# Pairwise feature interaction in fp32 on one core: transposes and weighing of a group issued together, last four rows stored by single partitions, other slot counts

## The reference

```
bilinear = jnp.einsum('bie,ied->bid', feature, weight)
out      = jnp.einsum('bid,bjd->bij', bilinear, feature)
```

## Time and profile before

| | |
|---|---|
| median of three runs | 1572.7 us |
| the profiled execution | 1573.6 us |
| its span, first to last instruction | 1571.8 us |
| TensorE matmul busy | 1525.3 us, 97% |
| VectorE busy | 1145.3 us, 73% |
| ScalarE busy | 928.2 us, 59% |
| DMA, mean busy share of the 16 engines | about 90% |
| HBM read, written | 108 MB, 328 MB |
| TensorE clock granted | 0.996 of full speed |

### The profile page before, as it was taken

How to read it: one execution, slowest core, us unless ns; L and a number is a source line. 1 busy time by engine, 2 the same in 40 slices (tenths; PEclk the granted TensorE clock), 3 DMA queues, 4 the chain that set the end, 5 groups by cost and what they waited for, 6 DMA issues and landing times.

```text
span 1571.8 us, 40835 instructions
## 1 busy us (share of the span) xinstructions
PE 1525.3 (97%) x16192; PEld 1209.0 (77%) x16192; DVE 1145.3 (73%) x2048; ACT 928.2 (59%) x1313; POOL 0.7 (0%) x6
## 2 busy tenths in 40 slices
PE   8999999999999999999999999999999999999974
PEld 6888778877788777887778877788777887788753
DVE  0567777777777778678787687777777777786896
ACT  5666556655566655665556655566555665556532
POOL 0000000000000000000000000000000000000000
PEclk9999999999999999999999999999999999999998
DMA  9788999889989999989999899899999989999788
GB/s 234 226 270 267 297 295 282 280 268 293 296 275 288 281 293 283 292 275 277 288 289 292 274 281 296 275 289 280 290 290 283 286 273 290 288 280 289 239 266 248
DMA packets 294235, 438.51 MB, mean 279 GB/s; under 512 B 38049, under 2 KB 242849, under 8 KB 294049
## 3 DMA queue, kind: packets, MB, share of 16 engines
q1 hardware_dynamic: 294048, 435.92, 89.8%
HBM read 108.13 MB, written 327.68 MB: 277 GB/s over the span
## 4 chain that ended last, share of the span: by engine, by line
PE 88%; DVE 8%; issue 2%; DMA 1%; SPq 0%; ACT 0%; DVEq 0%
PE ps L219 49%; PE bp L203 24%; PE tp L187 14%; DVE staging L250 4%; DVE win L298 2%; DVE win L305 1%; PE ps L203 1%; PE ps L187 1%; DMA x<-feature_dram 0%; DMA out_dram<-staging 0%; DVE win L306 0%; SPq L138 0%; SPq L131 0%; ACT staging L250 0%; ACT bl L272 0%
## 5 line engine op out<-in xcount | busy, mean ns | idle before, releaser
L219 PE MATMUL ps<-win,bl 64*100 64x200 f32 x8192 | 932.3, 354 | 24.1 <-DVE staging L250 23.9
L219 PEld LDWEIGHTS ps<-win,bl 64*100 64x100 f32 x8192 | 699.7, 207 | 167.6 <-issue 164.7
L250 DVE COPY staging<-ps 100x800 f32<-100x800 f32 x512 | 505.8, 988 | 326.7 <-PE ps L219 324.6
L272 ACT COPY bl<-bp 128x512 f32<-128x512 f32 x384 | 322.3, 839 | 449.7 <-PE bp L203 449.7
L250 ACT COPY staging<-ps 100x800 f32<-100x800 f32 x512 | 423.1, 826 | 164.9 <-PE ps L219 162.9
L203 PE MATMUL bp<-xt,w 64*64 64x128 f32 x6144 | 419.7, 276 | 0.0
L203 PEld LDWEIGHTS bp<-xt,w 64*64 64x64 f32 x6144 | 326.8, 133 | 83.5 <-ACT xt L263 78.7
L298 DVE COPY win<-xt 128x400 f32<-128x400 f32 x512 | 276.7, 541 | 63.4 <-ACT xt L263 47.5
L187 PE MATMUL tp<-ident,x 128*128 128x128 f32 x1536 | 252.8, 287 | 5.9 <-DMA x<-feature_dram 5.9
L187 PEld LDWEIGHTS tp<-ident,x 128*128 128x128 f32 x1536 | 161.6, 141 | 89.3 <-issue 89.1
L263 ACT COPY xt<-tp 128x512 f32<-128x512 f32 x384 | 226.6, 590 | 5.3 <-PE tp L187 5.3
(11 more groups left out here) (4 smaller groups left out, 0.4 us busy)
## 6 DMA issues: line engine op xcount, KB each, us to landing
out_dram<-staging SPq DMA_DIRECT2D x1024, 300.0 KB, 4.1
x<-feature_dram SPq DMA_DIRECT2D x400, 256.0 KB, 4.1
out_dram<-staging SPq DMA_DIRECT2D x512, 25.0 KB
w<-weight_dram SPq DMA_DIRECT2D x24, 128.0 KB, 5.6
w<-weight_dram SPq DMA_DIRECT2D x2, 64.0 KB, 4.4
```

The lines of the kernel that those rows point to most:

```text
L219: last = nc.tensor.matmul(ps[s % TILES][0:FH, h, F * b:F * (b + 1)], rows_of_bl(n, R * k + PB * i + b)[64 * h:64 * h + 64], win[64 * h:64 ...
L250: copy(staging[:, slot, :, :, :].rearrange("p b h j -> p h b j"), ps[s % TILES][0:FH, :, 0:PB * F].rearrange("p h (b j) -> p h b j", j=F)) ...
L272: nc.scalar.copy(group_of_bl(n, t), bilinear_tile(n, t).rearrange("p (c b) -> p c b", c=C)).then_inc(bl_stored, 1)
```

## The change

Five edits.

1. In a quad with preparation TensorE issues both score sets first, then the transposes, then the weighing.
2. The last four partitions are stored once for eight sets (REST = 8), by four transfers of one partition each with 16 pieces of 1600 B. Before it was once for two sets, by one transfer of four partitions. In both there are 512 such transfers with 25 KB each. Their landing semaphores now stand for eight slots.
3. OSLOTS goes from 12 to 16.
4. To make room, XSLOTS goes from 6 to 5 and WSLOTS from 4 to 3.
5. `store_bl` of an odd block walks through the group with the four features innermost, so that it reads PSUM with a step of 128 elements and writes four contiguous elements at a time. Before it read contiguously and wrote with a step of 128.

```diff
-    XSLOTS = 6
+    XSLOTS = 5
     TILES = 3
-    OSLOTS = 12
-    WSLOTS = 4
+    OSLOTS = 16
+    REST = 8
+    WSLOTS = 3
...
-        rest_written = [sem(f"rest_written{i}") for i in range(OSLOTS // 2)]
+        rest_written = [sem(f"rest_written{i}") for i in range(OSLOTS // REST)]
...
-            return bl[:, :, C * t:C * (t + 1)].rearrange("p b c -> p c b")
+            return bl[:, :, C * t:C * (t + 1)]
...
-                if s % 2:
+                if s % REST == REST - 1:
                     wait_staged(sp, s - 1)
-                    sp.dma_start(out_v[FA:FH, PB * (s - 1):PB * (s + 1), :],
-                                 staging[FA:FH, slot - 1:slot + 1].rearrange("p s b h j -> p (s b) (h j)")
-                                 ).then_inc(rest_written[slot // 2], 16)
+                    for p in range(FA, FH):
+                        sp.dma_start(out_v[p:p + 1, PB * (s + 1 - REST):PB * (s + 1), :],
+                                     staging[p:p + 1, slot + 1 - REST:slot + 1].rearrange(
+                                         "p s b h j -> p (s b) (h j)")
+                                     ).then_inc(rest_written[slot // REST], 16)
...
                     scores(n, k, 0)
+                    scores(n, k, 1)
                     if k in transposed_at and (n + 1) * NG + transposed_at[k] < BLOCKS * NG:
                         transposes((n + 1) * NG + transposed_at[k])
-                    scores(n, k, 1)
                     if k in weighed_at and n + 1 < BLOCKS:
                         bilinear(n + 1, weighed_at[k])
...
-                engine.wait_ge(rest_written[slot // 2], 16 * used)
+                engine.wait_ge(rest_written[slot // REST], 16 * (FH - FA) * used)
...
-                nc.scalar.copy(group_of_bl(n, t), bilinear_tile(n, t).rearrange("p (c b) -> p c b", c=C)
+                cells = "p (c b) -> p c b" if n % 2 == 0 else "p (c b) -> p b c"
+                nc.scalar.copy(group_of_bl(n, t), bilinear_tile(n, t).rearrange(cells, c=C)
```

More of the change, by code:

```diff
@@ L41, in feature_interaction @@
     assert 2 * E == 128 and B % NB == 0 and FH % C == 0 and NG <= QUADS and R == 2 * PB
-    assert PB * F <= 512 and C * NB == 512 and OSLOTS % 2 == 0
+    assert PB * F <= 512 and C * NB == 512 and OSLOTS % REST == 0 and (BLOCKS * SETS_B) % OSLOTS == 0
     feature_v = feature.rearrange("b f e -> b (f e)")
@@ L165, in _ @@
                 sp.wait_ge(out_written[slot], 16 * uses)
-                if slot % 2:
-                    sp.wait_ge(rest_written[slot // 2], 16 * uses)
+                if slot % REST == REST - 1:
+                    sp.wait_ge(rest_written[slot // REST], 16 * (FH - FA) * uses)
         @block.gpsimd
```

## The result

The changed kernel takes 1660.3 us, the median of four runs (1657.75 to 1671.62), against 1573.4 for the kernel before: a ratio of 1.057 with an interval of 1.052 to 1.062. It is 5.7% slower, where the prediction said 4% faster. The profiled execution spans 1660.5 us.

A forecast was written before the change was run, and what follows sets the result against it. TensorE's order of work was taken as the bound, with the DMA engines close behind. Terms -79 + 19 - 6 + 0.5 = -65.5 on a 1571.8 us span gave 1506, a median of 1507 us; range 1486 to 1525.

The forecast's parts named there:

- The order on TensorE: Score sets directly after one another in quads with transposes and weighing save 0.26 or 0.175 us each: -79 us.
- The drain's term: After TensorE ends, the last stores finish sooner if DMA keeps up: -6 us, bounds -8 and 0.
- WSLOTS 4 to 3: With three windows TensorE waits 1.3 us for window copies at each of 15 block ends: +19 us.
- ScalarE's other walk: ScalarE's `bl` copy of 1.07 us takes 0.59 to 1.07; covered by ScalarE's room, so 0 us.
- The sum without the rest stores: Total with rest stores costing nothing, DMA staying covered: 1507 us.
- The rest stores: Single-partition stores use 16 engines, each with 25 packets a quad, 2.18 us or 2.82 with a load; DMA stays covered.
- The rival on the other side: Rest stores run one packet after another, 1.39 us each: 2071 us, or about 1850 by the port limit; chance 6%.
- The engines' balance: Before, rest stores used four engines, carrying 28 output packets a quad against 24: 2.44 us a quad, 3.08 with a load.
- The DMA rival: All engines or memory limit the stretches where SP was behind, so DMA becomes the bound: 1545 us, chance 20%.
- XSLOTS: Feature slots 6 to 5: loads keep enough lead over store landing, small cost while block 0 is prepared: +0.5 us.

The follow-up runs named there:

- e9: The kernel before with the new order on TensorE and no rest stores (rows 96 to 99 of each half not written): 1486.6 us.
- i2: The changed kernel with its four rest stores in a row issued by GpSimd instead of SP, each reading 16 source partitions (wrong rows): 1507.4 us.
- e4: The changed kernel without any rest stores (4% of the output not written): 1506.7 us.
- i1: The changed kernel with its four single-partition rest stores in a row issued by GpSimd instead of SP, true source: 1624.6 us.
- e3: The changed kernel with the same four rest stores issued by SP, each reading 16 source partitions instead of one (wrong rows): 1660.1 us.
- e8: The changed kernel with one rest store of four partitions, 16 pieces each, once in eight sets, in place of four single-partition stores: 1742.1 us.
- g2: The kernel before with the new order on TensorE and its rest stores issued by ScalarE, one quad late, instead of SP: 1490.6 us.
- e5: The kernel before with the new order on TensorE and nothing else changed: 1542.0 us.
- e1: The changed kernel with the rest store of before (four partitions, four pieces each, after every second set): 1541.9 us.

## Why the prediction was wrong, point by point

- **The order on TensorE: right.** A quad takes 3.25 us as worked out. e9 is 86.5 us under the kernel before. Its drain, from TensorE's end (1475.09 + 3.28) to the end of the span at 1484.7, takes 6.3 us (6.5 in i2, with all stores), against 15.2 before. So 78 are left for the order, where I had 79. The drain's term was -6 and measures -9 here; in the changed kernel itself the drain takes 15.4 us, nothing less than before.
- **WSLOTS 4 to 3: right.** +19 forecast; e4 against e9 shows 20.0, though with both other slot counts and ScalarE's walk in it. The waits for VectorE's copies into `win` appear as said (34.5 us).
- **ScalarE's other walk: right to cost at nothing.** Its copy fell from 1.07 us to 0.586, and ScalarE wasn't the bound.
- **The sum without the rest stores: right.** 1507 forecast, 1506.7 in e4, and 1507.4 in i2 with all stores but another source.
- **The rest stores: the step that failed.** It read "On 16 engines each has 25 packets a quad: 2.18 us without and 2.82 with a load". I had the number of engines right (44,192 packets against 44,193 forecast). But I gave a piece out of one partition the 0.087 us of any other piece, and I gave the issue nothing at all. In its place i1 and i2 show that this source costs 117 us in 512 stores, 0.23 us a store. And e3 against i2 shows that the burst of issues in SP's queue, 3.2 us for four, costs 153 us by itself.
- **The rival on the other side had the right mechanism.** "The partition serves them in turn" is near what the holes show, except that the four partitions share the rate (e8). At 28 to 31 GB/s the 16 pieces of a store take 0.83 to 0.91 us, an estimate from these windows, where the rival had 1.39. The port rule of the Trainium skill (SBUF — State Buffer, Door 1) gives these four partitions 27.2 GB/s together, and the trace agrees: 28 to 31 in the changed kernel, 27 in e8. The 1850 us worked out from it are too many: 0.94 us for each of 512 stores are 481 us, where the holes of 2.5 us sum to 320. I gave the case 6% because four partitions had served "4 pieces at a time without ruin". e8 shows that this holds for 16 pieces and not for 64, so the evidence didn't carry that far.
- **The engines' balance: a wrong reading of the earlier trace rows.** I took 2.44 us a quad and a share of 0.86 for four full engines. g2 leaves each rest store on four engines with the same pieces, and the kernel runs at TensorE's pace, 51 us under e5. What changed is the queue, and that each store goes one quad later. So, as far as g2 shows, 3.08 and 2.44 us a quad were not what four full engines need, but the pace of one queue with rest stores among the main ones. The DMA rival's 1545 us from these rows fits e1 and e5 (1542), for that other reason.
- **XSLOTS: nothing where I costed it, larger elsewhere.** The first scores start at 51.4 us, 1.1 us later than in the earlier trace rows, but in e5, with six slots, they start at 51.8. So this isn't the slots' doing. But the loads stand behind the stores in SP's queue, and a late SP means missing features: 88 us of TensorE's waits. That I took only the landing time against the slots' lead, and not SP's lag, is part of the same failed step.

What stays open is why the rest stores of before cost 51 us in SP's queue and 4 in ScalarE's: the time that SP is held (a median of 0.91 us for each in e5, 0.26 for ScalarE's in g2) or the order in which an engine takes two queues. A sign is that in e5 the staging copies wait 91 us for rest stores to land (84.5 on ScalarE, 6.8 on VectorE), and in g2 not at all. No run takes the reasons apart.

## What to carry to other kernels

Before pieces are moved to fewer partitions to spread a transfer over more DMA engines, look at where they are read: engines that together read one partition, or the four neighbours of this case, wait for it, and the main stores wait behind them, even where the two kinds come from different queues (i1). A small transfer also costs its issue; keep it out of the queue that feeds the engines, if another engine has the room, and not four in a row there either. When two suspected causes stand at one place, taking one away can show nothing: look at whether the engines in the hole are stuck or idle, and take both away.

## What the runs showed of the hardware that I had not expected

- The shortest issue of a store that has 16 pieces in one partition takes 0.50 us of SP; one of four partitions with four pieces 0.26 us, and one of 96 partitions with 300 KB 0.32 us. The row of the changed kernel's L151 (min/median/max ns), then that of before's L147:

```profile
L151 SPq DMA_DIRECT2D out_dram<-staging x512: 502/597/1687, 64.3 to 1656.7; - x171
```

```profile
L147 SPq DMA_DIRECT2D out_dram<-staging x512: 260/670/2072, 54.3 to 1567.4; - x171
```

- The last four partitions gave 28 to 31 GB/s to 16 engines that read one of them at a time, and 27 to four engines that read one each (e8).
- A DMA engine's busy share can be high because it waits for its source: 0.76 at 28 GB/s, where 1.00 goes with 327.
- With the rest stores on ScalarE's queue, the core held 295 GB/s over the whole span, 16 more than before, with no other shape of any transfer.
